# First layer's attention: maximum scans folded into the averaging loop, weights scaled on ScalarE, k products ahead of v, last products on GpSimd

## The reference, cut to what matters

```python
h = _ln(x, ln1_w, ln1_b);  hx = _shift(h)           # hx: h one token earlier
xk = h * tmk + hx * (1.0 - tmk)                      # the same for xv, xr
k, v = xk @ att_kw.T, xv @ att_vw.T
sr = sigmoid(xr @ att_rw.T)
def step(carry, kv):                                 # w = -exp(time_decay), u = time_first
    p = maximum(pp, u + kk);  e1 = exp(pp - p);  e2 = exp(u + kk - p)
    out = (e1 * aa + e2 * vv) / (e1 * bb + e2)
    p2 = maximum(pp + w, kk); e1b = exp(pp + w - p2); e2b = exp(kk - p2)
    return (e1b * aa + e2b * vv, e1b * bb + e2b, p2), out
x = x + (sr * out) @ att_ow.T
h = _ln(x, ln2_w, ln2_b)                             # the feed-forward follows
```

## Time and profile before

| | |
|---|---|
| median of three runs | 1258.63 us (1257.43 to 1260.14) |
| the profiled execution | 1258.89 us, span 1257.1 us |
| TensorE matmul busy | 988.2 us (79%) |
| VectorE busy | 921.3 us (73%) |
| ScalarE busy | 638.2 us (51%) |
| GpSimd busy | 599.4 us (48%) |
| TensorE's mean granted clock | 0.92 |
| DMA over the span | 61.22 MB, mean 49 GB/s |

### The profile page before, as it was taken

The page is one execution under the profiler, slowest core; times in us unless marked ns, Lnnn a source line. Parts: engine busy times, 40 slices in busy tenths (PEclk is TensorE's granted clock), DMA queues, the critical chain, the costliest instruction groups (busy, mean ns, idle before and its releaser), DMA issues.

```text
span 1257.1 us, 12629 instructions
## 1 busy us (share of the span) xinstructions
PE 988.2 (79%) x3048; PEld 560.2 (45%) x3048; DVE 921.3 (73%) x1229; ACT 638.2 (51%) x1157; POOL 599.4 (48%) x432
## 2 busy tenths in 40 slices
PE   5849888388878984599999999876676776675896
PEld 2314343133326723488888888432222222224684
DVE  4684895999977568466666666587989998955564
ACT  4744657300054483255555555776555555453455
POOL 3010275566630033277777777303656565623572
PEclk9979899599998996699999999987989998997899
DMA  2000300000020000476666666000000000000661
GB/s 72 1 0 0 111 0 15 0 0 1 0 59 0 1 16 7 92 156 152 146 142 155 151 147 156 3 0 1 0 0 0 0 0 0 1 13 15 149 153 34
DMA packets 18639, 61.22 MB, mean 49 GB/s; under 512 B 2560, under 2 KB 12416, under 8 KB 12800
## 3 DMA queue, kind: packets, MB, share of 16 engines
q1 hardware_dynamic: 18608, 60.86, 20.7%
HBM read 59.15 MB, written 1.70 MB: 48 GB/s over the span
## 4 chain that ended last, share of the span: by engine, by line
PE 48%; DVE 34%; issue 6%; ACT 5%; POOL 4%; DMA 2%; DVEq 1%; SPq 0%; POOLq 0%; ACTq 0%
PE ps L351 46%; DVE g L1378 5%; DVE g L1177 4%; DVE tmp L1177 4%; DVE y L1628 3%; DVE g L1628 2%; ACT rstd L759 2%; ACT g L759 2%; DVE resid L1177 2%; DVE parts L1317 2%; DVE parts L1177 2%; POOL g L1164 2%; DVE g L1585 1%; POOL sq L1068 1%; DMA g<-coef_scratch 1%
## 5 line engine op out<-in xcount | busy, mean ns | idle before, releaser
L351 PE MATMUL ps<-parts 128*128 128x512 f32 x1800 | 449.8, 408 | 34.1 <-DVE g L1177 10.0
L351 PEld LDWEIGHTS ps<-parts 128*128 128x128 f32 x1800 | 345.1, 194 | 137.8 <-DVE parts L1177 17.9
L759 ACT ACTIVATE g<-ps 128x512 f32<-128x512 f32 (+4 forms) x310 | 183.0, 597 | 314.7 <-PE ps L351 285.1
L1107 POOL TENSOR_TENSOR parts<-g,parts 128x512 fp32r<-128x512 f32 x168 | 217.6, 1295 | 156.2 <-ACT parts L759 152.2
L1164 POOL TENSOR_TENSOR g<-g 128x1024 f32<-128x1024 f32 x64 | 150.3, 2353 | 137.9 <-ACT g L759 134.9
L351 PE MATMUL ps<-g,arena 128*128 128x512 f32 (+1 forms) x328 | 164.9, 645 | 62.0 <-POOL g L1151 23.5
L1177 DVE TENSOR_TENSOR ps<-g,ps 128x512 f32<-128x512 f32 x168 | 116.9, 696 | 112.6 <-PE ps L351 90.7
L759 ACT ACTIVATE parts<-g 128x512 fp32r<-128x512 f32 (+2 forms) x252 | 126.3, 534 | 30.9 <-DVE g L1177 15.8
L351 PEld LDWEIGHTS ps<-g,arena 128*128 128x128 f32 (+1 forms) x328 | 62.3, 201 | 162.9 <-issue 61.0
L1177 DVE TENSOR_TENSOR g<-ps,g 128x512 f32<-128x512 f32 x160 | 110.7, 692 | 32.7 <-DMA g<-coef_scratch 14.9
L1068 POOL TENSOR_TENSOR sq<-resid 128x512 f32<-128x512 f32 x32 | 35.9, 1122 | 198.5 <-DVE resid L1177 185.0
(11 more groups left out here) (172 smaller groups left out, 1067.7 us busy)
## 6 DMA issues: line engine op xcount, KB each, us to landing
g<-coef_scratch SPq DMA_DIRECT2D x80, 512.0 KB, 6.2
g<-in_moe_dram SPq DMA_DIRECT2D x42, 192.0 KB, 4.9
g<-in_rope_dram SPq DMA_DIRECT2D x1, 2048.0 KB, 8.5
arena<-in_weights_dram SPq DMA_DIRECT2D x1, 1348.5 KB, 5.8
arena<-in_weights_dram SPq DMA_DIRECT2D x1, 1028.5 KB, 4.8
g<-in_x_dram SPq DMA_DIRECT2D x4, 256.0 KB, 4.0
out_dram<-g SPq DMA_DIRECT2D x4, 256.0 KB, 2.5
arena<-in_weights_dram SPq DMA_DIRECT2D x1, 838.0 KB, 6.9
```

The costliest lines, as they stand in the source:

```text
L351: return nc.tensor.matmul(o, lhsT, rhs, start=start, stop=stop, **kw)
L759: return nc.scalar.activation(o, i, func, **kw)
L1107: pv.tensor_tensor(hid_lo[:, cols(c)], g[:, 6, (c % 2) * N:(c % 2 + 1) * N], hid_hi[:, cols(c)].bitcast(F32), ALU.subtract).then_inc(s["hl ...
```

## The change

ScalarE takes over the weights: VectorE only makes `1 - amount` (three numbers per channel), and does it, with the negated identity and the negated biases, before its first large operation; ScalarE scales the six matrices before "pre0"'s rstd. TensorE's two bias products go ahead of `variance("ln1")`. k(0) and k(1) go first, then per chunk k(c+1), less_last_max(c), v(c). max(0) and max(1) stand ahead of the averages, max(c+2) inside avg(c) behind its second scan. GpSimd multiplies sr by the reciprocal of the denominator, so that VectorE has one product per chunk instead of two; the first add to x stands ahead of the fourth product.

```diff
 TensorE
+            mm(ps[:, 7, 0:1], W(0, "vw"), W(0, "vec", 1, 2))
+            mm(ps[:, 7, 1:2], W(0, "rw"), W(0, "vec", 1, 2)).then_inc(s["bias_bank"], 1)
             variance("ln1", 0)
...
+            pe.wait_ge(s["rest_ready"], 1)
             pe.wait_ge(s["mixed_ready"], 1)
-            pe.wait_ge(s["bias_ready"], 1)
-            for c in range(CHUNKS):
-                pe.wait_ge(s["h1_ready"], c + 1)
-                pe.wait_ge(s["rstd_ready"], CHUNKS * (NORM["ln1"] + 1))
-                shifted(ps[:, c, :], "kw", c).then_inc(s["k_bank"], 1)
-                if c:
-                    less_last_max(c - 1)
+            k_of(0)
+            for c in range(CHUNKS):
+                if c + 1 < CHUNKS:
+                    k_of(c + 1)
+                less_last_max(c)
+                if c == CHUNKS - 1:
+                    pe.wait_ge(s["bias_ready"], 1)
                 shifted(ps[:, 4 + c, :], "vw", c).then_inc(s["v_bank"], 1)
-            less_last_max(CHUNKS - 1)
 ScalarE, behind the copies of y
+            act.wait_ge(s["w_loaded"], 16)
+            f(small[:, 15:16], W(0, "vec", 10, 11), ACT.Exp).then_inc(s["decay_ready"], 1)
+            act.wait_ge(s["rest_ready"], 1)
+            for w, k in (("kw", 4), ("vw", 5), ("rw", 6)):
+                f(now_w[w], W(0, w), ACT.Copy, scale=W(0, "vec", k, k + 1))
+                last = f(last_w[w], W(0, w), ACT.Copy, scale=rest_of[w])
+            last.then_inc(s["mixed_ready"], 1)
             rstd_of("pre0", eps5, 0)
 GpSimd, ahead of token_shift
+            for c in range(CHUNKS):
+                pool.wait_ge(s["sr_ready"], c + 1)
+                pool.wait_ge(s["rd_ready"], c + 1)
+                pv.tensor_tensor(G(7, c), G(7, c), y[:, cols(c)], ALU.mult).then_inc(s["srd_ready"], 1)
 VectorE, ahead of the first centred chunk
             dve.wait_ge(s["consts_loaded"], 16)
+            v.tensor_scalar(neg_ident[:, :], ident, -1.0, None, ALU.mult)
+            dve.wait_ge(s["w_loaded"], 16)
+            for w, amount in (("kw", tmk), ("vw", tmv), ("rw", tmr)):
+                v.tensor_scalar(rest_of[w], amount, -1.0, 1.0, ALU.mult, ALU.add)
+            v.tensor_scalar(neg_bonus, bonus, -1.0, None, ALU.mult)
+            chain(v.tensor_scalar(g[:, 0, 0:1], ln1_b, -1.0, None, ALU.mult))
+            chain.wait()
+            dve.sem_inc(s["rest_ready"], 1)
 VectorE, behind the multiplication of "pre0"
-            for w, amount in (("kw", tmk), ("vw", tmv), ("rw", tmr)):
-                v.tensor_scalar(now_w[w], W(0, w), amount, None, ALU.mult)
-                chain(v.tensor_scalar(last_w[w], W(0, w), amount, None, ALU.mult))
-            chain.wait()
-            for w in ("kw", "vw", "rw"):
-                v.tensor_tensor(last_w[w], W(0, w), last_w[w], ALU.subtract)
+            v.tensor_scalar(w_decay, small[:, 15:16], -1.0, None, ALU.mult).then_inc(s["decay_negated"], 1)
 in the averages, behind the second scan
+                if c + 2 < CHUNKS:
+                    running_max(c + 2)
 behind the averages
-                chain(tt(G(4, c), G(4, c), y[:, cols(c)]))
-                chain.wait()
-                dve.wait_ge(s["sr_ready"], c + 1)
+                dve.wait_ge(s["srd_ready"], c + 1)
                 tt(G(4, c), G(4, c), G(7, c)).then_inc(s["rw_ready"], 1)
...
+            running_max(0)
+            running_max(1)
+            for c in range(CHUNKS):
+                average(c)
+            gated(0)
+            gated(1)
+            gated(2)
+            add_to_x(0)
+            gated(3)
+            for c in range(1, CHUNKS):
+                add_to_x(c)
```

More of the change, by code:

```diff
@@ L144, in sandwich @@
             dve_chain act_chain zeroed raw_ready
-            h1_ready d_ready mix_ready k_bank v_bank r_bank sr_ready pp_ready mixed_ready bias_bank bias_ready
+            h1_ready d_ready mix_ready k_bank v_bank r_bank sr_ready pp_ready rest_ready decay_negated mixed_ready bias_bank bias_ready srd_ready
             kd_bank kd_used eb_clipped eb_ready ee_ready den_ready rd_ready rw_ready decay_ready ow_bank x1_ready
@@ L235, in sandwich @@
         last_w = {w: derived(0, 256 * i + 128, 256 * i + 256) for i, w in enumerate(("kw", "vw", "rw"))}
+        rest_of = {w: small[:, 56 + i:57 + i] for i, w in enumerate(("kw", "vw", "rw"))}
         v_bias, r_bias, neg_bonus = small[:, 53:54], small[:, 54:55], small[:, 55:56]
@@ L394, in _ @@
             variance("pre0", 0)
+            pe.wait_ge(s["w_loaded"], 16)
+            pe.wait_ge(s["x_ready"], CHUNKS)
+            mm(ps[:, 7, 0:1], W(0, "vw"), W(0, "vec", 1, 2))
+            mm(ps[:, 7, 1:2], W(0, "rw"), W(0, "vec", 1, 2)).then_inc(s["bias_bank"], 1)
             variance("ln1", 0)
@@ L406, in less_last_max, with k_of @@
                 mm(ps[:, c, :], neg_ident[:, :], G(8, c, 0), False, True, skip_group_check=True).then_inc(s["kd_bank"], 1)
[L408 to L411, removed]
+            def k_of(c):
+                pe.wait_ge(s["h1_ready"], c + 1)
+                shifted(ps[:, c, :], "kw", c).then_inc(s["k_bank"], 1)
+            pe.wait_ge(s["rest_ready"], 1)
             pe.wait_ge(s["mixed_ready"], 1)
-            pe.wait_ge(s["bias_ready"], 1)
+            k_of(0)
             for c in range(CHUNKS):
-                pe.wait_ge(s["h1_ready"], c + 1)
-                pe.wait_ge(s["rstd_ready"], CHUNKS * (NORM["ln1"] + 1))
-                shifted(ps[:, c, :], "kw", c).then_inc(s["k_bank"], 1)
-                if c:
-                    less_last_max(c - 1)
+                if c + 1 < CHUNKS:
[3 more added lines that the diff above has]
+                    pe.wait_ge(s["bias_ready"], 1)
                 shifted(ps[:, 4 + c, :], "vw", c).then_inc(s["v_bank"], 1)
-            less_last_max(CHUNKS - 1)
             for c in range(CHUNKS):
@@ L791, in _ @@
                 f(y[:, cols(c)], ps[:, c, :], ACT.Copy).then_inc(s["y_ready"], 1)
+            act.wait_ge(s["w_loaded"], 16)
[5 more added lines that the diff above has]
+            last.then_inc(s["mixed_ready"], 1)
             rstd_of("pre0", eps5, 0)
             rstd_of("ln1", eps5, 0)
-            act.wait_ge(s["w_loaded"], 16)
-            f(small[:, 15:16], W(0, "vec", 10, 11), ACT.Exp).then_inc(s["decay_ready"], 1)
             act.wait_ge(s["bias_bank"], 1)
@@ L800, in _ @@
             f(r_bias, ps[:, 7, 1:2], ACT.Copy).then_inc(s["bias_ready"], 1)
-            act.wait_ge(s["mixed_ready"], 1)
+            act.wait_ge(s["decay_negated"], 1)
             def clipped_exps(c, slot, over, under, used, done):
@@ L1202, in _ @@
                 v.memset(small[:, k:k + 1], value)
-            v.memset(g[:, 0, 0:1], 0.0)
             v.memset(g[:, 8, 0:1], -1e38)
@@ L1207, in _ @@
             v.memset(small[:, 51:52], 0.0).then_inc(s["zeroed"], 1)
+            vec = [W(0, "vec", k, k + 1) for k in range(12)]
+            ln1_w, ln1_b, ln2_w, ln2_b, tmk, tmv, tmr, bonus, f_tmk, f_tmr = vec[:10]
+            w_decay = small[:, 14:15]
             dve.wait_ge(s["consts_loaded"], 16)
+            v.tensor_scalar(neg_ident[:, :], ident, -1.0, None, ALU.mult)
[6 more added lines that the diff above has]
+            dve.sem_inc(s["rest_ready"], 1)
             for c in range(CHUNKS):
@@ L1214, in _ @@
             scale_by_rstd("pre0", H, R, "h_ready")
-            vec = [W(0, "vec", k, k + 1) for k in range(12)]
-            ln1_w, ln1_b, ln2_w, ln2_b, tmk, tmv, tmr, bonus, f_tmk, f_tmr = vec[:10]
-            w_decay = small[:, 14:15]
             dve.wait_ge(s["decay_ready"], 1)
-            chain(v.tensor_scalar(w_decay, small[:, 15:16], -1.0, None, ALU.mult))
-            dve.wait_ge(s["w_loaded"], 16)
-            for w, amount in (("kw", tmk), ("vw", tmv), ("rw", tmr)):
-                v.tensor_scalar(now_w[w], W(0, w), amount, None, ALU.mult)
-                chain(v.tensor_scalar(last_w[w], W(0, w), amount, None, ALU.mult))
-            chain.wait()
-            for w in ("kw", "vw", "rw"):
-                v.tensor_tensor(last_w[w], W(0, w), last_w[w], ALU.subtract)
-            v.tensor_scalar(neg_ident[:, :], ident, -1.0, None, ALU.mult)
-            v.tensor_scalar(neg_bonus, bonus, -1.0, None, ALU.mult)
-            v.tensor_scalar(g[:, 0, 0:1], ln1_b, -1.0, None, ALU.mult).then_inc(s["mixed_ready"], 1)
+            v.tensor_scalar(w_decay, small[:, 15:16], -1.0, None, ALU.mult).then_inc(s["decay_negated"], 1)
             for c in range(CHUNKS):
@@ L1240, in mix, with running_max @@
                 return v.scalar_tensor_tensor(o, G(1, c), amount, G(0, c, 0), ALU.mult, ALU.add)
-            for c in range(CHUNKS):
+            def running_max(c):
                 dve.wait_ge(s["k_bank"], c + 1)
@@ L1245, in _, with average @@
                     dve.wait_ge(s["pp_ready"], c)
+                else:
+                    dve.wait_ge(s["decay_negated"], 1)
                 v.tensor_tensor_scan(G(8, c, 1), w_decay.to_broadcast([P, N]), ps[:, c, :],
```

(16 more changed lines are left out.)

## The result

The changed kernel takes 1244.43 us, median of four runs (1242.38 to 1245.68), against 1258.13 us for the kernel before beside it. The ratio is 0.9879 (95% interval 0.9859 to 0.9899), that is 15.2 us less (12.7 to 17.7). A second measurement gave 0.9873 (0.9855 to 0.9890). I had forecast 12.4 us and a range of 1244.0 to 1250.0 us.

The account below looks back on a forecast made before the run. First-layer attention was taken as bound by VectorE, then TensorE's order, then VectorE: avg(0) 15.2 us earlier, less 2.4 for scans and 1.2 for contention, leaving 12.4 saved with rounding, 1246.2 us against the median; range 1244.0 to 1250.0.

Parts of the forecast that it names:

- Preparation: Before the first norms: VectorE's small instructions, ScalarE's Exp and scalings (at most 2.0 us) and the bias products are free.
- First average: Start of avg(0) on VectorE: at 32.5 instead of 47.67 us, 15.2 us earlier.
- that rival: TensorE's clock falls anyway at k(0) and k(1), behind the variances: 8 us saved, 1250.4 us; chance 0.07.
- Averages with scans: VectorE's four averages with max(2) and max(3) inside the first two: 2.4 us longer, the last ending at 60.8.
- Products: GpSimd's products of sr and reciprocal overlap VectorE's averages twice, 0.6 us each: +1.2 us, bounds 0 and 1.7.
- the reciprocals end last: Slow r products delay ScalarE's reciprocals, so VectorE waits for GpSimd: 9.5 to 10.5 us saved, 1248.1 to 1249.1; chance 0.13.
- Output products: TensorE's eight output records, starting at 62.75 instead of 75.14, again take 5.66 us; bounds -2.1 and +1.5.
- The stage: First layer's attention, up to VectorE's last add to x: 12.4 us shorter.
- unmoved: A DMA load of fixed time swallows the 12.4 us and the end stays at 1258.6 us; chance 0.03.
- slower: TensorE's clock falls more in later stages, at mean 0.895 making the kernel 3 us slower, 1262 us; chance 0.02.
- From the end mark on the same work follows: Everything behind VectorE's last add to x at 81.52 us is unchanged, put at no gain or loss.
- a sign that I am wrong: Stages behind the last add changing by more than 2 us, one of three signs listed against the forecast.

Follow-up runs that it names:

- idle maxima: Two or four unread VectorE maxima added ahead of the feed-forward's mixes: changed kernel 0.9896 and 0.9909, kernel before 0.9994 and 1.0000, all against the kernel before.
- the Exp ahead: Kernel before with one edit, ScalarE's Exp of the decay moved ahead of its norms: ratio 0.9953 to the kernel before.
- filled pauses: Changed kernel with TensorE's two pauses filled by overwritten products: 0.9876 to the kernel before; with the last products also back on VectorE, 0.9884.

## Why the prediction was right and where it failed

- *Preparation.* Right. The six scalings take 0.39 us each, but overlap, so that Exp and scalings are done in 2.0 us (12.49 to 14.44) and hide. The Trainium skill (ScalarE: Activation LUTs, What ACT_TABLE_LOAD costs) states figures from which one with a scale from memory is estimated at 186 + 93 + 0.833 x 128 = 386 ns. The trace agrees (0.39 us); the row I took has 0.30. The bias products hide too: behind them TensorE still waits 0.58 us for squares.
- *First average.* Forecast 15.2 us earlier, measured 15.0 (35.57 - 20.59). k(0) follows the variances, and the clock does not fall there (1.00 from 27 to 30 us); that rival is out.
- *Averages with scans.* Forecast +2.4, measured 2.36: the four take 28.32 us, from 34.30 to 61.92 + 0.69, against 25.96 before, four periods of 6.46 and 0.1 for the last add's tail.
- *Products.* I took 1.2 us of contention inside the averages and 0.75 from there to the first output product, 1.95 in all. Measured: none inside and 2.97 behind (62.61 to 65.58) in the first profile, 0.5 and 1.73 in the second. That the sum held is in part luck: a wait of 1.23 us for GpSimd stood where I had put 1.2 us of contention. My bound for one overlap, 0.8 us, was too small: it is 1.0. The rival "the reciprocals end last" was half true. TensorE waits 4.32 us for max(3) in both profiles; the two records behind the wait took 2.07 us in the first and 1.19 in the second, r came 0.9 us later in the first, and VectorE waited 1.23 us there and not at all in the second.
- *Output products.* 5.66 taken, 5.67 measured in both profiles. That is luck too: with the same code they took 6.7 us in both profiles with idle maxima.
- *The stage.* 12.4 forecast, 11.2 and 12.2 measured.
- *Slips that move nothing.* 8 us saved from 1258.6 is 1250.6, not 1250.4. The chances of "unmoved" and "slower" are 0.03 and 0.02 in the list and the other way round in the sum by outcome. The 0.64 us held against GpSimd's 1.04 are of adds that read PSUM; a product of two SBUF tensors takes VectorE 0.69.
- *The step that failed* is "From the end mark on the same work follows", put at nothing. It is the same work, and it is 3.7 to 4.7 us shorter, where more than 2 us was to be a sign that I am wrong. Busy time of one stretch of the same later stage, before and then after, from the same matmul on (columns as in the earlier trace rows, the clock third from the end):

```profile
930.00:1010.00 80.00, 57.86 (x134) 22.28 (x134) 73.64 (x64) 41.47 (x87) 50.32 (x22) 0.92 0.00 0
```

```profile
920.00:998.00 78.00, 53.57 (x138) 20.63 (x139) 74.94 (x66) 42.76 (x90) 51.97 (x23) 1.00 0.00 0
```

and the second profiles of both:

```profile
930.00:1010.00 80.00, 57.64 (x134) 22.35 (x135) 73.68 (x64) 42.20 (x89) 50.28 (x22) 0.91 0.00 0
```

```profile
918.00:996.00 78.00, 53.64 (x138) 20.69 (x139) 74.94 (x66) 42.68 (x90) 51.97 (x23) 1.00 0.00 0
```

Before, TensorE is at 1.2 GHz for some 13 of the 80 us (mean 0.92 and 0.91) and does 134 matmuls in them; after, it is at 2.4 GHz throughout (1.00) and does 138 in 78. By the starts of corresponding matmuls the stretch is 3.6 us shorter, in both pairs of profiles; the other stretches give and take up to 1.9 us and nearly cancel. VectorE goes from 92% busy to 96%, so it had waited for TensorE there. I had this mechanism among the rivals, only with the sign of a loss, and had argued against it with the spread of three runs of one kernel. That spread says nothing of the patterns that another kernel takes.

Shown: one edit of the first stage (products on GpSimd) shortens the rest without touching it, by the ratio of twelve executions as well as by the profile (1175.6 to 1170.5), and 1.3 and 2.1 us of added work vanish behind it. With the Exp ahead the profile has 1171.2, but it is the fastest of six executions (1250.54 us, median 1252.34), and its ratio less its stage leaves between 3.5 us shorter and 0.8 us longer.

Not settled: what in the first stages sets the pattern, and how often a kernel takes which. With the clock's falls there filled up, the rest became 2 to 3 us shorter and its stretches changed pattern too. That fits with the meeting of the work and the clock's changes as the cause, but no run fixed that meeting and varied nothing else.

## What to carry to other kernels

Before moving work off an engine, look at what that engine waited for: here one Exp of 0.19 us behind another engine's long queue held the weights, and moving it gave more than moving the weights. A product handed to GpSimd while VectorE works on two SBUF tensors was no parallel work here, so look for places where VectorE is idle or reads PSUM: beside the squares for "pre0" VectorE's instructions on PSUM kept their 0.68 us and GpSimd's its 1.04. And where TensorE's clock falls in many short pauses, a change of an early stage can change the time of untouched later ones, here by up to 5 us; a forecast of 1% should carry that much on either side.

## What the runs showed of the hardware that was not expected

- VectorE and GpSimd, each with two SBUF inputs of 128x512, cost each other as much as if they took turns: alone 0.69 and 1.04 us, together 1.64 to 1.75 for VectorE and up to 1.72 for GpSimd. The sum of the two alone is 1.73. The Trainium skill (GPSIMD Engine Reference, Key points) names the contention; the trace agrees, and puts it at the whole of it.
- A VectorE scaling of 128x128 with one SBUF input took 0.99 and 1.08 us beside GpSimd and 0.27 alone, almost four times as long.
- The time of the unchanged later stages (kernels with filled pauses left out) differed between profiles by up to 5.8 us (1169.8 to 1175.6). Two profiles of the kernel before agreed to 0.03 us, but 63 executions of it had mean granted clocks of 0.920 to 0.925 and times 6.1 us apart.
